# Adding gathered rows to a sum on TensorE instead of VectorE, in the first edge pass of a graph network

## The reference, cut to what matters

```python
def _L0_gnn_ref(x, edge_index, edge_attr, u, batch, W1, b1, W2, b2):
    src, dst = edge_index[0], edge_index[1]
    u_per_node = u[batch]
    all_feat = jnp.concatenate([x[dst], x[src], edge_attr, u_per_node[dst]], axis=-1)
    msg = jax.nn.relu(all_feat @ W1 + b1)
    agg = jax.ops.segment_sum(msg, dst, num_segments=x.shape[0])
    node_in = jnp.concatenate([x, agg, u_per_node], axis=-1)
    return jax.nn.relu(node_in @ W2 + b2)
```

## Time and profile before

| | us |
|---|---|
| time, median of 3 runs (12688.62 to 12696.25) | 12688.88 |
| the profiled execution's own time | 12692.79 |
| its span, first to last instruction | 12691.0 |
| busy: PE 6733.1, PEld 5780.0, DVE 4907.3, ACT 395.8 | |
| busy: POOL | 9386.9 |

### The profile page before, as it was taken

One profiled execution on the slowest core, in us unless ns is written; L12 is line 12 of the kernel. 1 busy time (PEld: TensorE's weight loads), 2 busy tenths in 40 slices (PEclk: granted clock), 3 DMA queues, 4 the chain that ended last, 5 costly groups with the idle time before them and its releaser, 6 DMA issues.

```text
span 12691.0 us, 121543 instructions
## 1 busy us (share of the span) xinstructions
PE 6733.1 (53%) x29865; PEld 5780.0 (46%) x29865; DVE 4907.3 (39%) x12980; ACT 395.8 (3%) x790; POOL 9386.9 (74%) x9927
## 2 busy tenths in 40 slices
PE   4888877888878833333333333343333333333334
PEld 4777766677767733333333333333333333333333
DVE  2444444444444333333333333333333333333334
ACT  0000000000000100000000000000000000000000
POOL 6777777777777577777777777767777777777774
PEclk9666667666666555555555555555555555555555
DMA  2444434343444222222222222221111111111111
GB/s 78 100 94 93 95 93 96 92 95 92 98 94 94 65 41 40 41 40 40 40 40 40 41 40 40 40 54 27 27 27 27 27 27 27 27 27 27 27 27 37
DMA packets 1598914, 688.43 MB, mean 54 GB/s; under 512 B 1359841, under 2 KB 1422977, under 8 KB 1598734
## 3 DMA queue, kind: packets, MB, share of 16 engines
q0 software_dynamic: 315680, 328.70, 13.3%
q1 hardware_dynamic: 1283181, 359.10, 12.8%
HBM read 658.74 MB, written 28.14 MB: 54 GB/s over the span
## 4 chain that ended last, share of the span: by engine, by line
POOL 32%; PE 28%; DMA 19%; issue 15%; DVEq 3%; DVE 2%; POOLq 0%; ACT 0%; SPq 0%; ACTq 0%
POOL message L556 30%; PE sum_ps L666 20%; DMA message<-source_table,index 18%; PE pre_ps L642 3%; DVEq L920 3%; PE pre_ps L639 2%; POOL fetched L574 1%; DVE by_rank L952 1%; POOL ranked L538 1%; DVE summed_in L931 0%; PE out_ps L701 0%; PE out_ps L703 0%; PE out_ps L702 0%; PE sum_ps L689 0%; DMA xt<-in_x_t 0%
## 5 line engine op out<-in xcount | busy, mean ns | idle before, releaser
L556 POOL DMA_INDIRECT message<-source_table,index x9375 | 8887.3, 948 | 2947.0 <-issue 2546.7
L666 PE MATMUL sum_ps<-hit,message 128*64 128x128 f32 (+1 forms) x18750 | 4254.6, 408 | 4821.3 <-DMA message<-source_table,index 4746.6
L666 PEld LDWEIGHTS sum_ps<-hit,message 128*64 128x64 f32 (+1 forms) x18750 | 3577.4, 231 | 5348.2 <-DMA message<-source_table,index 4962.0
L952 DVE TENSOR_TENSOR by_rank<-by_rank,sum_ps 64x128 f32 (+1 forms) x9375 | 2628.5, 280 | 4567.1 <-PE sum_ps L666 4277.6
L937 DVE TENSOR_TENSOR hit<-out_ps,edge_place 128x640 f32<-128x640 f32 x1875 | 1526.8, 814 | 1207.2 <-PE sum_ps L666 690.6
L639 PE MATMUL pre_ps<-w_edge,scratch 96*128 96x192 f32 x2500 | 946.9, 473 | 874.6 <-DVE summed_in L931 742.0
L642 PEld LDWEIGHTS pre_ps<-scratch 128*128 128x128 f32 x6250 | 1230.9, 271 | 111.5 <-issue 79.0
L642 PE MATMUL pre_ps<-scratch 128*128 128x64 f32 x6250 | 1278.4, 356 | 0.0
L639 PEld LDWEIGHTS pre_ps<-w_edge,scratch 96*128 96x128 f32 x2500 | 525.5, 262 | 1119.3 <-DVE summed_in L931 790.6
L931 DVE TENSOR_TENSOR summed_in<-pre_ps,message 128x320 f32<-128x320 f32 x625 | 303.1, 485 | 771.7 <-issue 594.1
L925 DVE TENSOR_SCALAR scratch<-edge_cat,lane 128x640 f32<-128x640 bf16 x625 | 344.9, 552 | 603.2 <-issue 593.1
(11 more groups left out here) (153 smaller groups left out, 1270.3 us busy)
## 6 DMA issues: line engine op xcount, KB each, us to landing
message<-source_table,index POOLq DMA_INDIRECT x9375
edge_cat<-place_rows SPq DMA_DIRECT2D x125, 800.0 KB
scratch<-ranked SPq DMA_DIRECT2D x3125, 32.0 KB
scratch<-in_edge_t_steps SPq DMA_DIRECT2D x125, 480.0 KB, 4.6
message<-in_edge_steps SPq DMA_DIRECT2D x625, 80.0 KB, 2.5
xt<-in_x_t SPq DMA_DIRECT2D x28, 224.0 KB, 3.6
index<-in_src_steps SPq DMA_DIRECT2D x375, 12.5 KB
fetched<-sums,node_idx POOLq DMA_INDIRECT x294, 2.5
```

The source lines that it names most:

```text
L556: nc.gpsimd.indirect_dma_start(to, None, source_table[l][:, :], bass.IndirectOffsetOnAxis(ap=index[:, at.j, s:s + 1], axis=0))\
L666: one = mm(tile_sum(at.half, s)[0:w, :], of, hit[:, at.half, s, :], start=True, stop=True)
L952: V.tensor_tensor(at_rank[s], at_rank[s], tile_sum(at.half, s)[0:w, :], ALU.add)\
```

## The change

In pass 0 `before_relu` gets a first matmul: the identity is the stationary operand, the 320 gathered columns of the step are the moving one, and the result opens the accumulation in the half of `pre_ps`; the other matmuls accumulate behind it. For that TensorE waits in `before_relu` for the gathered rows of its step. VectorE's add, its tile `summed_in` and the semaphore `added` go. ScalarE waits for `pre_done` and takes the relu from PSUM. TensorE waits for `message_made` before it writes a half of `pre_ps` again, and GpSimd waits for `pre_done` before it fills a slot of the ring again.

```diff
--- before.py
+++ after.py
@@ -133,7 +133,6 @@
         spread = part(2 * S * P).rearrange("p (u s e) -> p u s e", u=2, s=S)
         assert at <= NB * F and NB * F + TILES <= SCRATCH and TURNS * TURN * S * P // 2 <= NB * (C + 2)
         hit = sb("hit", [P, 2, S, P])
-        summed_in = sb("summed_in", [P, 2, S, F])
         message = sb("message", [P, RING, S, W0])
         ring = message.rearrange("p u s w -> p (u s w)")
         rows = ring[:, 0:RING * S * F].rearrange("p (u s f) -> p u s f", u=RING, s=S)
@@ -224,7 +223,6 @@
         hit_made = [sem(f"hit_made{l}") for l in range(3)]
         by_rank_cleared = sem("by_rank_cleared")
         pre_done = sem("pre_done")
-        added = sem("added")
         message_made = sem("message_made")
         terms_kept = sem("terms_kept")
         tile_summed = [sem(f"tile_summed{l}") for l in range(3)]
@@ -545,7 +543,7 @@
             for l in range(3):
                 def steps(at, l=l):
                     if l == 0:
-                        wait(pool, added, at.number - RING + 1)
+                        wait(pool, pre_done, at.number - RING + 1)
                     else:
                         wait(pool, tile_summed[l], at.number - RING + 1)
                     if at.part == 0:
@@ -629,18 +627,21 @@
                 pe.compute_val(m.number - 1)
                 pe.compute_val(m.number + 1)
                 pe.compute_val(m.turn * (16 * S) + 16 * S)
-                wait(pe, added, m.number - 1)
+                wait(pe, message_made, m.number - 1)
                 pe.wait_ge(spread_made, m.number + 1)
                 pe.wait_ge(window_in[m.part], m.turn * (16 * S) + 16 * S)
                 if m.part == 0:
                     pe.wait_ge(eat_in[m.j // TURN], m.index_loads(0))
+                wait_for_rows(pe, m, 0)
+                mm(pre_ps[:, m.half, 0:S * F], ident[:, :], rows[:, m.slot, :, :].rearrange("p s f -> p (s f)"),
+                   start=True, stop=False)
                 for q in range(0, S, STACK):
                     n = min(STACK, S - q)
                     mm(pre_ps[:, m.half, q * F:(q + n) * F], eat[0:n * C, m.j // TURN, m.part, q // STACK, :],
-                       w_edge[0:n * C, 0:n * F], start=True, stop=False)
+                       w_edge[0:n * C, 0:n * F], start=False, stop=False)
                     for s in range(q, q + n):
                         one = mm(pre_ps[:, m.half, s * F:(s + 1) * F], spread[:, m.half, s, :], window[:, m.part, s, :],
-                                 start=False, stop=(s == q + n - 1))
+                                 start=False, stop=(s == S - 1))
                 one.then_inc(pre_done, 1)
 
             for l in range(3):
@@ -745,10 +746,10 @@
 
                 def steps(at, l=l):
                     if l == 0:
-                        act.wait_ge(added, at.number + 1)
+                        act.wait_ge(pre_done, at.number + 1)
                         wait(act, tile_summed[0], at.number - 1)
                         nc.scalar.activation(active[:, at.half, :, :],
-                                             summed_in[:, at.half, :, :], ACT.Relu).then_inc(message_made, 1)
+                                             pre_ps[:, at.half, 0:S * F].rearrange("p (s f) -> p s f", f=F), ACT.Relu).then_inc(message_made, 1)
 
                 wait_for_table(act, l)
                 if l == 0:
@@ -924,14 +925,6 @@
                         wait(dve, pre_done, o.number - 1)
                         V.tensor_scalar(spread[:, o.half, :, :].rearrange("p s e -> p (s e)"), place_row[:, o.j // TURN, o.part, :],
                                         lane[:, 0:1], None, ALU.is_equal).then_inc(spread_made, 1)
-                    if l == 0 and m.real:
-                        dve.wait_ge(pre_done, m.number + 1)
-                        wait_for_rows(dve, m, l)
-                        wait(dve, message_made, m.number - 1)
-                        V.tensor_tensor(summed_in[:, m.half, :, :],
-                                        pre_ps[:, m.half, 0:S * F].rearrange("p (s f) -> p s f", f=F),
-                                        rows[:, m.slot, :, :], ALU.add)\
-                            .then_inc(added, 1)
                     if m.real:
                         wait(dve, tile_summed[l], m.number - 1)
                         V.tensor_tensor(hit[:, m.half, :, :], over(along_ps, [P, S, P], 1),
```

## The result

The changed kernel takes 12,711.25 us (median of 20 runs, 12,705.74 to 12,718.4), the kernel before 12,688.63 us (20 runs, 12,681.25 to 12,696.25): ratio 1.0017, with a 95% interval from 1.0011 to 1.0024. Measured again later, the pair gave 1.0014 (1.0005 to 1.0023). So the change makes the kernel a little slower, by 17 to 23 us. Both ratios lie inside the 0.2% that was counted as no change, the upper ends of both intervals just outside it.

What follows compares the result with a forecast made beforehand. GpSimd, issuing gathers without ever waiting, was taken to bound pass 0. All terms were 0 except the tail's +6 us: 12,692.8 + 6 = 12,698.8, about 12,695 as median of runs; range 12,668 to 12,740.

Steps and rivals of the forecast that it cites:

- VectorE's add costs nothing where it goes: On VectorE in pass 0: 625 adds, 306 us, go; GpSimd doesn't wait for them and they lengthen no gather: 0 us.
- ScalarE: ScalarE's relu reading PSUM: its 0.47 us at most stay, 0 us in the steady state.
- The identity matmul: On TensorE in before_relu: 0.65 or 1.2 us more, steps of 4.0 or 7.4 us; clock rises, TensorE keeps up: 0 us.
- The index loop: Index loads for GpSimd: before_relu ends 12 to 14 us later against the gathers, 10 of 24 us stay: 0 us.
- The tail: Work behind pass 0's last gather, hidden by nothing: +3.9 to +9.4 us, taken as +6.
- The phase of the spread: Where in a gather VectorE's spread starts, which can lengthen that gather: 0, with 20 us either way as likely.
- rival B: Spreads fall into a worse phase of the gathers: 20 to 60 us slower, 12,715 to 12,755 us; chance 0.11.
- The sign written for a shift: Pass 0's mean gather outside 957 ± 7 ns would show that spreads fell into a worse or better phase.
- Rival C: Spreads fall into a better phase: 12,653 us with all 42 us gone, 12,674 with half; chance 0.06 beyond 25 us.
- rival A's milder form: TensorE 11 us or more late at turns, so indices come late: 20 to 100 us; most of rival A's 0.10.

## Why the prediction was right, and where not

12,695 us were forecast, within 0.2% of before at 0.73, and 12,668 to 12,740 as a range. 12,711 came, +0.17%, on the near side of that line by 3 us. The mechanism was right, that GpSimd's gathers bound pass 0 and only their length and the tail can change; that the result stayed under 0.2% is in part luck, since the larger of its two terms was put at 0.

1. *VectorE's add costs nothing where it goes.* Held: no gather waited before, none waits now. The add's 306 us (257 of them in 400 to 4200 us) are gone from VectorE, and no time was gained by it.
2. *ScalarE.* Held: 0.44 us from PSUM for 0.47.
3. *The identity matmul.* 0.65 and 1.2 us were put in. From its start to the next matmul's it takes 0.61 us at the upper clock and 1.22 at the lower; steps without waits take 3.92 and 7.27 us (4.0 and 7.4). TensorE kept up, and its clock rose to 0.76 (0.72 to 0.85 forecast), far above the 0.60 at which it would have been late. TensorE now waits 380 us for landed gathers in 400 to 4200 us, 166 times, and its clock is higher all the same. The waits take the place of those for the add, and all its waits together are fewer: 633 us where it was 729. By the Trainium skill (TensorE: Matmul & The Clock Gate, section "Loop structure matters more than you think") TensorE goes cold in a loop with a long DMA wait between every matmul. This loop isn't that one, and the prediction left out the word long: only 166 of some 600 steps wait for a gather, 2.3 us on average and 5.8 at most, and the trace neither bears the rule out nor contradicts it. TensorE's waits in 400 to 4200 us (total, times, longest), in the kernel before:

```profile
PE pre_ps L639 <- DVE summed_in L931: 725.2, 248, 6.9
```

and in the changed one:

```profile
PE pre_ps L636 <- DMA message<-source_table,index: 380.0, 166, 5.8
PE pre_ps L636 <- issue: 129.7, 42, 4.4
PE pre_ps L636 <- DVE scratch L926: 116.1, 40, 4.3
```

4. *The index loop.* `before_relu` was to end 4.3 to 6.6 us behind its gathers. The median is 7.8 and the latest 15.2: I had left out TensorE's lateness in long stretches at the lower clock, though it stood in the same paragraph as a risk. The 70th index load and the first gather that needs it, to be laid beside the earlier trace rows (24 us apart):

```profile
2467.78 0.39 SPq L407 DMA_DIRECT2D index<-in_src_steps  x1
```

```profile
L554 POOL DMA_INDIRECT message<-source_table,index x1724: 940/945/1452, 297.5 to 2482.8; - x192
```

15 us are left (the 1726th gather of the pass starts at 2482.8; the window misses the first two). The smallest distance from the end of an index load's issue to its first gather in the pass is 4.6 us (6.2 in the later execution). In the kernel before it was 16.7, so the 24 us of the turn that the prediction looked at were near the median (24.6) and not the worst case. No row shows how long such a load takes to land. No gather waited, so the cover was there, and thinner than the 10 us argued.

5. *The tail.* +6 was taken, +6.4 and +5.3 came, by the steps named. The working left out the sum of step 623 and its tile sums, which also stand behind the last rows; they run beside the tile sums of step 622 and the last hit, and hold the last tile sums up by only 0.3 us.

6. *The phase of the spread* is the step that was mis-sized: 0 was put in, +18 and +13 came. Both lie inside the 20 us either way that stood beside the 0, and just under rival B's 20 to 60, but the value rested on a wrong sentence, "It still drifts ... so I stay at today's mean". An even drift over all places doesn't give today's mean. It gives the mean over the places, 58 us by the table above, and today's 42 were a favourable set: 27 of 100 spreads fell on the free stretch of 0.1 to 0.3 us, and 19 of 100 on the dearest. Now they are 16 and 32 of 100, which isn't even either. The sign written for a shift, a mean gather outside 957 ± 7 ns, didn't show it (963 ns), since 7 ns a gather are 22 us. Had I priced the places in the trace of before and taken their mean, the forecast would have been 12,695 + 16 = 12,711; that it would have come so near is luck, as 56 and 60 us in two executions of one kernel don't show that a kernel in general comes out at the mean, and the kernel before didn't. That the growth is this phase is shown by the excess, nearly all of it in gathers over which a spread lies, by the prices, nearly alike in three traces, and by the PSUM spreads, with which it goes; the run that should have turned the last into time, where GpSimd never waits, is missing. Why the spreads moved just so was not taken apart further.

Rival C (a better phase) was out, and rival A's milder form, late indices, didn't occur in the result or its repeat. Late indices did occur where the sequencers are slow, in each kernel traced there, those made from the kernel before too, so the change isn't what causes them; with a TENSOR_TENSOR spread the change cost some 40 to 50 us there.

## What to carry to other kernels

Taking work from an engine for which nobody waits gains nothing, and moves all that is timed by it: look for what its instructions do to the bound engine at each phase. Price the places one by one; where nothing says how they will shift, the mean over them is a better guess than today's share (here 58 us, for 60 and 56 measured and 42 before). Where gathers that GpSimd issues are the bound, look for VectorE operations that lengthen them: here a one-source operation from SBUF and one with two operands in SBUF did, and one with an operand in PSUM didn't. That this saves time where GpSimd never waits is a forecast, and where it waited the kernels got slower by it. A new wait in the queue of an in-order engine lengthens the tail by all that stands behind it.

## What the hardware showed that was not expected

A VectorE TENSOR_SCALAR of 640 columns from bf16 in SBUF (0.54 us) lengthens a gather's issue on GpSimd by 0 to 0.3 us on average at a place (stretches of 0.05 us, the dearest 1.1 to 1.15 us behind its start, 295 ns in both kernels), and a TENSOR_TENSOR with both operands in SBUF (0.81 us) by up to 0.6, depending on where in the gather it begins; the worst single gathers gain 0.51 us (1452 ns for 944) and 0.83 us (1769), about the whole length of the operation; one of 0.81 us with an operand in PSUM does nothing (longest gather 961 ns). The Trainium skill (SBUF — State Buffer, section "SBUF: two separate sides") has the lock for both forms (for two SBUF inputs against a GpSimd operation that reads SBUF) and says that the loser fully blocks. These traces agree on the forms and on the worst gathers, but a gather is blocked only from some places of it, and for many spreads hardly at all (68 of 100 in the kernel before and 48 in the changed one cost less than 50 ns). And the same program takes 28 to 29% longer on three of the four chips of the experiments (16,204 to 16,414 us for 12,690). In pass 0 there SP and TensorE have stretches of some 20 us in a turn with 0.7 us for a register instruction; that these make up the whole of it wasn't shown.
